# Four-layer graph and expert network on one core: last stage searches in two token halves, third expert stage finishes tiles singly, third graph layer loads bias rows first

## The reference

```python
x = x + _L0_gnn_ref(_layernorm(x), ...)   # and so on, gnn and ffn for 0, 1, 2, 3
```

```python
h = jax.nn.relu(jnp.einsum('bsd,bfd->bsf', x, W1m) + b1m[:, None, :])
res = x + jnp.einsum('bsf,bdf->bsd', h, W2m) + b2m[:, None, :]
mu = res.mean(axis=-1, keepdims=True)
var = res.var(axis=-1, keepdims=True)
return (res - mu) * jax.lax.rsqrt(var + LN_EPS) * lng + lnb
```

```python
Sm = jax.nn.softmax(xf @ W_router + b_router, axis=-1)
G_ek, idx_ek = jax.lax.top_k(Sm.T, k)          # 32 experts, 39 tokens each
tokens = xf[idx_ek]
up = jnp.einsum('gjkh,ghf->gjkf', tok_g, W_up) + b_up[:, None, None, :]
Eout = jnp.einsum('ekf,efh->ekh', silu(up), W_down) + b_down[:, None, :]
y = zeros.at[idx_ek.reshape(-1)].add((G_ek[..., None] * Eout).reshape(-1, H))
```

## Time and profile before

| | us |
|---|---|
| median of 3 runs | 2931.55 (2931.22 to 2933.32) |
| profiled execution, its own time | 2929.89 |
| its span (first to last instruction) | 2928.1 |
| PE busy | 2461.4 (84%) |
| DVE busy | 1624.7 (55%) |
| ACT busy | 837.2 (29%) |
| POOL busy | 585.8 (20%) |
| mean DMA rate over the span | 150 GB/s |

### The profile page before, as it was taken

How to read it: one execution, slowest core, us unless ns; L and a number is a source line. 1 busy time by engine, 2 the same in 40 slices (tenths; PEclk the granted TensorE clock), 3 DMA queues, 4 the chain that set the end, 5 groups by cost and what they waited for, 6 DMA issues and landing times. The chain is left out here.

```text
span 2928.1 us, 31276 instructions
## 1 busy us (share of the span) xinstructions
PE 2461.4 (84%) x10766; PEld 1562.6 (53%) x10766; DVE 1624.7 (55%) x3768; ACT 837.2 (29%) x1860; POOL 585.8 (20%) x563
## 2 busy tenths in 40 slices
PE   3899947999957999985568899999999869958877
PEld 1355446999944777774443455344554434434443
DVE  9999353132424889986246898627963354431100
ACT  0155011111112776771111465105641110101110
POOL 0000065455303555420110000000000101012211
PEclk9899957999977999996789999999999989979988
DMA  4000363776724555543443553214541331459996
GB/s 135 0 1 27 120 187 100 260 230 217 260 73 131 155 156 155 152 88 128 125 137 121 194 193 106 89 62 138 189 132 54 127 138 46 144 195 337 347 347 222
DMA packets 195434, 440.43 MB, mean 150 GB/s; under 512 B 25179, under 2 KB 45387, under 8 KB 194798
## 3 DMA queue, kind: packets, MB, share of 16 engines
q1 hardware_dynamic: 156958, 344.67, 35.1%
q0 software_dynamic: 38320, 93.76, 12.3%
HBM read 394.21 MB, written 43.93 MB: 150 GB/s over the span
## 5 line engine op out<-in xcount | busy, mean ns | idle before, releaser
L2124 PE MATMUL psum<-x_res,HH 125*128 125x512 f32 (+1 forms) x960 | 351.7, 525 | 20.2 <-DVE x_res L2314 20.2
L2124 PEld LDWEIGHTS psum<-x_res,HH 125*128 125x128 f32 x960 | 181.3, 193 | 179.8 <-issue 156.4
L1101 POOL DMA_INDIRECT recd<-edge_records,edge_slots x160 | 193.1, 1207 | 293.8 <-issue 287.2
L1468 POOL DMA_INDIRECT hg<-HT,srcidx x196 | 191.2, 975 | 258.5 <-PE psum L1589 128.6
L1630 ACT ACTIVATE hg<-hg,ex 128x129 f32<-128x129 f32 x784 | 235.2, 389 | 1.6
L1589 PE MATMUL psum<-hg,Dh 128*125 128x258 f32 x784 | 208.0, 424 | 6.8 <-DVE ACC L1531 4.3
L2114 PE MATMUL psum<-W,XO 128*125 128x512 f32 x480 | 209.0, 596 | 0.0
L2891 PE MATMUL psum<-wd,XN 128*40 128x512 f32 (+1 forms) x550 | 162.3, 621 | 31.6 <-DMA wd<-in_L_ffn_b_down 22.2
L1589 PEld LDWEIGHTS psum<-hg,Dh 128*125 128x125 f32 x784 | 160.1, 209 | 40.7 <-issue 6.8
L1135 PE MATMUL psum<-xgT,w 128*128 128x187 f32 x1024 | 172.8, 329 | 4.1 <-DMA w<-in_L_ffn_w 4.1
L1135 PEld LDWEIGHTS psum<-xgT,w 128*128 128x128 f32 x1024 | 166.2, 194 | 8.7 <-DMA w<-in_L_ffn_w 5.8
(11 more groups left out here) (520 smaller groups left out, 3977.0 us busy)
## 6 DMA issues: line engine op xcount, KB each, us to landing
w<-in_L_ffn_w SPq DMA_DIRECT2D x64, 1024.0 KB, 15.1
wd<-in_L_ffn_W_down SPq DMA_DIRECT2D x24, 2560.0 KB
MK<-CT SPq DMA_DIRECT2D x80, 625.0 KB, 3.8
wu<-in_L_ffn_W_up SPq DMA_DIRECT2D x8, 2730.0 KB, 16.4
wd_ahead<-in_L_ffn_W_down SPq DMA_DIRECT2D x6, 2560.0 KB
rows<-ROWS POOLq DMA_DIRECT2D x24, 625.0 KB, 7.2
w<-in_L_ffn_W SPq DMA_DIRECT2D x18, 512.0 KB
t<-in_L_ffn_tv_W SPq DMA_DIRECT2D x16, 512.0 KB
```

What stands on the lines that cost most here:

```text
L1101: pool.indirect_dma_start(out=g.recd, out_offset=bass.IndirectOffsetOnAxis(ap=g.posi[:, c:c + 1], axis=0), in_=g.E8[:, c, :], in_offset=No ...
L1468: pool.indirect_dma_start(out=hg[j % RING][:, c, :], out_offset=None, in_=g.HT, in_offset=bass.IndirectOffsetOnAxis(ap=g.srcidx[:, j * CH ...
L2124: return pe.matmul(flat[:, at:at + x1 - x0], HH[:, k, h * DH + c * 128:h * DH + c * 128 + 128], z[n % 4][:, x0:x1], start=(k == 0 and i < ...
```

## The change

Three edits that don't touch each other.

1. gnn2: the two loads of the bias rows are issued ahead of the mask and W1.
2. ffn2: `dve_group` and `dve_finish` are replaced by `dve_tile`, which finishes one tile after the other on DVE. ACT keeps only the square roots, one column each, and its pass over the tile is gone; the subtraction of the mean and the product with gamma are one instruction that reads PSUM, and the scaling and the sum with X another.
3. last_layers: the search. Tiles t and t + 5 of the routing weights are put beside each other (`self.at`), so that one transposition of 64 columns makes the rows of both halves: expert e of the first 625 tokens in row e, of the second in row 32 + e. Each half gives its largest 40. The list of the second half is turned around in its first 39 places; then slot j of the result is the larger of entry j of the first list and entry j of the turned second list, which together are the largest 39. Slot 40 is gathered still, but the scatter moves 39 rows. Some small tiles are placed in other rooms (`st` in g.ones, `choice` in g.iota_tp).

```diff
@@ class Router @@
+        self.at = list(range(NT))
...
+        self.at = [2 * (t % (NT // 2)) + t // (NT // 2) for t in range(NT)]
...
-        for t in range(NT):
-            ins = pe.transpose(g.PS[0:ne, t // 4, (t % 4) * TP:(t % 4 + 1) * TP], self.L[:, t, :],
-                               g.ident[0:TP, 0:TP])
+        for j in range(NT // 2):
+            ins = pe.transpose(g.PS[0:2 * ne, j // 4, (j % 4) * TP:(j % 4 + 1) * TP],
+                               self.L[:, 2 * j:2 * j + 2, :].rearrange("p a e -> p (a e)"), g.ident[0:TP, 0:TP])
...
+        for k, (first, second) in enumerate(((self.val, self.rval), (self.idf, self.rid))):
+            pe.transpose(g.PS[0:self.count, k, 0:ne], first[0:ne, :], g.ident[0:ne, 0:ne])
+            ins = pe.transpose(g.PS[0:self.count, 2 + k, 0:ne], second[ne:2 * ne, :],
+                               g.ident[ne:2 * ne, ne:2 * ne])
...
+        dve.tensor_copy(WT[:, 0:4 * TP], g.PS[0:2 * ne, 0, 0:4 * TP]).then_inc(*v.up())
+        dve.tensor_copy(WT[:, 4 * TP:5 * TP], g.PS[0:2 * ne, 1, 0:TP]).then_inc(*v.up())
...
+        dve.tensor_copy(self.rval[ne:2 * ne, 0:n], val[ne:2 * ne, n - 1::-1]).then_inc(*v.up())
+        dve.tensor_copy(self.rval[ne:2 * ne, n:], val[ne:2 * ne, n:]).then_inc(*v.up())
         step(dve.tensor_copy(idf[:], ix[:]))
-        step(dve.tensor_scalar(val[:], val[:], 0.0, None, ALU.max))
-        if self.kept < self.count:
-            step(dve.memset(val[:, self.kept:self.count], 0.0))
+        dve.tensor_scalar(self.rid[ne:2 * ne, 0:n], idf[ne:2 * ne, n - 1::-1], float(N // 2), None,
+                          ALU.add).then_inc(*v.up())
+        dve.tensor_scalar(self.rid[ne:2 * ne, n:], idf[ne:2 * ne, n:], float(N // 2), None, ALU.add).then_inc(*v.up())
...
+        dve.tensor_copy(self.sw[:], v1).then_inc(*v.up())
+        step(dve.tensor_copy(self.diff, t1))
+        dve.tensor_tensor(self.ge, v0, self.sw[:], ALU.is_ge).then_inc(*v.up())
+        step(dve.tensor_tensor(self.diff, t0, self.diff, ALU.subtract))
+        dve.tensor_tensor(self.sw[:], v0, self.sw[:], ALU.max).then_inc(*v.up())
+        step(dve.tensor_tensor(self.diff, self.diff, self.ge, ALU.mult))
+        dve.tensor_tensor(self.si[:], t1, self.diff, ALU.add).then_inc(*v.up())
@@ gnn2 @@
         def sp_program():
+            for l, b in enumerate((b1, b2)):
+                sp.dma_start(br[l * C8:(l + 1) * C8, :], b.rearrange("(c p) -> c p", p=128)).then_inc(*b_in.up(16))
             sp_mask(0)
             sp.dma_start(Wt[:, 0:KC, :], rows_of(W1)).then_inc(*w_in.up(16))
-            for l, b in enumerate((b1, b2)):
-                sp.dma_start(br[l * C8:(l + 1) * C8, :], b.rearrange("(c p) -> c p", p=128)).then_inc(*b_in.up(16))
@@ ffn2 @@
-            for i, (t0, t1) in enumerate(groups):
-                act.wait_ge(*var.at(i + 1))
-                act.activation(rs[:, t0:t1], rs[:, t0:t1], ACT.Sqrt).then_inc(*root.up())
-                act.wait_ge(*ready.at(i + 1))
-                for t in range(t0, t1):
-                    act.activation(XN[0:TP, t, :], g.PS[0:TP, t % 8, :], ACT.Identity, bias=nb[:, t:t + 1],
-                                   scale=rs[:, t:t + 1]).then_inc(*normed.up())
+            for t in range(NT):
+                act.wait_ge(*var.at(t + 1))
+                act.activation(rs[:, t:t + 1], rs[:, t:t + 1], ACT.Sqrt).then_inc(*root.up())
...
+        def dve_tile(t):
             step = Chain(dve, v)
...
+            one, res = slice(t, t + 1), g.PS[0:TP, t % 8, :]
+            dve.wait_ge(*down.at(t + 1))
+            step(dve.bn_stats(st[:, t, :], res))
+            step(dve.bn_aggr(mv[:, t, :], st[:, t, :]))
+            dve.tensor_scalar(rs[:, one], mv[:, t, 1:2], EPS, None, ALU.add).then_inc(*var.up())
+            dve.scalar_tensor_tensor(XN[0:TP, t, :], res, mv[:, t, 0:1], lng[:], ALU.subtract,
+                                     ALU.mult).then_inc(*normed.up())
+            dve.wait_ge(*root.at(t + 1))
+            dve.reciprocal(rs[:, one], rs[:, one]).then_inc(*ready.up())
+            dve.wait_ge(*normed.now())
+            dve.wait_ge(*ready.now())
+            step(dve.scalar_tensor_tensor(g.X[:, t, :], XN[0:TP, t, :], rs[:, one], g.X[:, t, :], ALU.mult, ALU.add))
+            tile_statistics(g, t)
@@ last_layers @@
-        rt.slots(SL, K, old[0:NE, 0:N])
+        rt.slots(SL, K, old[0:2 * NE, 0:N // 2], [g.iota_tp[0:SL, k * NE:(k + 1) * NE] for k in range(2)])
...
-                ap=rt.si[:, 0, e:e + 1], axis=0), in_=wo[:, e % (2 * GS), :], in_offset=None,
+                ap=rt.si[0:K, e:e + 1], axis=0), in_=wo[0:K, e % (2 * GS), :], in_offset=None,
```

More of the change, by code:

```diff
@@ L699, in dve_softmax, with slots @@
         dve.wait_ge(*self.v.now())
-    def slots(self, count, keep, WT=None):
+    def slots(self, count, keep, WT=None, choice=None):
         s, ne = self.s, self.ne
         self.count, self.kept = count, keep
[L704 to L710, removed]
+        self.at = [2 * (t % (NT // 2)) + t // (NT // 2) for t in range(NT)]
+        self.WT = WT if WT is not None else s.sb("weights_by_expert", [2 * ne, N // 2])[:]
+        self.ix = s.sb("top_index", [2 * ne, count], U32)
+        self.val, self.idf = s.sb("half_value", [2 * ne, count]), s.sb("half_token", [2 * ne, count])
+        self.rval, self.rid = s.sb("turned_value", [2 * ne, count]), s.sb("turned_token", [2 * ne, count])
+        self.ge, self.diff = choice if choice is not None else [s.sb(n, [count, ne])[:] for n in ("first_half", "between_halves")]
+        self.sw, self.si = s.sb("slot_w", [count, ne]), s.sb("slot_i", [count, ne], I32)
     def pe_slots(self):
@@ L727, in dve_slots @@
         dve, step, g, ne, v = self.g.nc.vector, Chain(self.g.nc.vector, self.v), self.g, self.ne, self.v
[L728 removed]
+        WT, ix, val, idf, n = self.WT, self.ix, self.val, self.idf, self.kept
         dve.nop().then_inc(*self.weights.up())
         dve.wait_ge(*self.turned.at(1))
[L731 to L733 removed]
+        dve.tensor_copy(WT[:, 0:4 * TP], g.PS[0:2 * ne, 0, 0:4 * TP]).then_inc(*v.up())
+        dve.tensor_copy(WT[:, 4 * TP:5 * TP], g.PS[0:2 * ne, 1, 0:TP]).then_inc(*v.up())
         dve.wait_ge(*v.now())
@@ L2569, in dve_merge @@
             dve.nop().then_inc(*w2_in.up())
-        def dve_group(i, t0, t1):
+        def dve_tile(t):
             step = Chain(dve, v)
[L2573 to L2588, removed]
-                dve.tensor_tensor(XN[0:TP, t, :], XN[0:TP, t, :], lng[:], ALU.mult).then_inc(*v.up())
-                dve.wait_ge(*v.now())
-                dve.tensor_tensor(g.X[:, t, :], g.X[:, t, :], XN[0:TP, t, :], ALU.add).then_inc(*v.up())
-                dve.wait_ge(*v.now())
-                tile_statistics(g, t)
+            one, res = slice(t, t + 1), g.PS[0:TP, t % 8, :]
[11 more added lines that the diff above has]
+            tile_statistics(g, t)
         def dve_program():
@@ L2601, in dve_program @@
             dve.wait_ge(*lnb_in.at(1))
-            dve_group(0, *groups[0])
-            for i in range(len(groups)):
-                if i + 1 < len(groups):
-                    dve_group(i + 1, *groups[i + 1])
-                dve_finish(i, *groups[i])
+            for t in range(NT):
+                dve_tile(t)
         sp_program()
@@ L2649, in last_layers @@
         inv, minus = s.sb("inv", [TP, NT]), s.sb("minus_inv", [TP, NT])
-        st, mv, rs = s.sb("st", [TP, NT, 6]), s.sb("mv", [TP, NT, 2]), s.sb("rs", [TP, NT])
+        st, mv, rs = view(g.ones, TP, 0, NT, 6), s.sb("mv", [TP, NT, 2]), s.sb("rs", [TP, NT])
         vectors = s.sig("vectors_loaded")
@@ L2986, in dve_rows @@
                     dve.wait_ge(*scattered.at(16 * (e - 2 * GS + 1)))
-                dve.tensor_scalar(row, g.PS[place[k], 4 + k, :], rt.sw[:, 0, e:e + 1], None,
+                dve.tensor_scalar(row, g.PS[place[k], 4 + k, :], rt.sw[:, e:e + 1], None,
                                   ALU.mult).then_inc(*ev.up())
```

16 lines of the change are left out of this document (5 added, 11 removed).

## The result

The changed kernel took 2903.02 us (median of 4 runs, 2900.26 to 2908.33), the kernel before 2932.44 beside it (4 runs, 2931.22 to 2935.25): a ratio of 0.9906, interval 0.9892 to 0.992. It is 29.4 us faster; 27.5 were forecast (a median of 2904, from 2931.55), and the range of 2898 to 2912 held it. The profiled execution took 2900.26 us with a span of 2898.2, against 2928.1 before.

The account below looks back on a forecast made before the run. Ten barrier-ended stages bound the kernel by what each waits for: bias rows in gnn2, DVE in ffn2, the search in the last. Savings 8.1 + 9.6 + 9.8 = 27.5 us gave 2904 us, range 2898 to 2912.

Parts of the forecast that it names:

- Part 1: gnn2, bias rows first: 7.0 us of PE idleness and 1.9 of clock, less 0.8: 8.1 us saved (6.1 to 8.9).
- the later store: gnn2: POOL's store of attention rows, issued 8.9 us earlier, meets the loads' end; cost 0.8 us, between 0 and 2.8.
- Part 2: ffn2, tiles finished singly on DVE: 3.3 us per tile, 33.1 for ten against 42.7, 9.6 us saved (7.7 to 10.7).
- the root is covered: ffn2: ScalarE's square root runs under DVE's first product (0.74 us); uncovered it would add some 0.3 us per tile.
- Part 3: Last stage, search in halves: 1.0 + 0.8 + 9.2 - 1.2 = 9.8 us saved (8.2 to 10.9).
- the turning: Last stage: PE transposes five pairs of routing-weight tiles instead of ten tiles, saving 1.0 us.
- the copies: Last stage: copies of the turned weights from PSUM fall from 1.72 to 0.93 us, saving 0.8.
- the search: Last stage: fourteen DVE maxima, index searches and replacements over 625 columns, not 1250, save 9.2 us (8.0 to 10.2).
- the merge: Last stage: joining both halves' lists takes seven more small instructions and two more PE transpositions, adding 1.2 us (0.7 to 1.8).
- The copy's slope: Last stage: the PSUM copies' 1.06 ns per column, taken to price search operations at 0.66 us saved each.
- The weight stream: Rival, last stage: the expert-weight stream sets the end by itself, so the search's gain is lost: 2914 us, chance 0.05.
- a fortieth less is nothing: Last stage: scattering 39 rows, not 40, gains nothing; by the skill's rule, 0.2 us per last scatter, half a microsecond overall.

Follow-up runs that it names:

- one pair of kernels: The changed kernel with its 39-row scatters, against the changed kernel with all 40 slots scattered, sent together: 2899.68 and 2905.36 us.

## Why the prediction was right

- **Part 1** gave 7.5 us in the profiled run, 7.9 alone, of the 8.1 forecast, within its 6.1 to 8.9. Idle time (7.0) and clock (1.8) came as worked out; the second was shown by keeping PE busy. The term that was mis-sized is the later store: 0.8 taken, 1.6 measured (4.21 less 2.59), because the traffic that it meets is not only the end of the loads but also the store of X, as the run that holds that store back showed. DVE's first maximum came 7.3 us nearer to the stage's start, where the prediction named 8 to 9. DVE's path, not PE's, sets the end: PE waits for its AB steps, by 1.05 and 2.07 us. That is no sure mark of the change, though: two kernels with the old order show such a wait too (1.87 us in the one with tiles singly, 0.43 in the one with the search in halves).
- **Part 2** gave 9.5 of 9.6 us, at 3.3 us a tile. That the root is covered holds; without that cover it cost 0.27 a tile (the bound said 0.3).
- **Part 3** gave 9.7 of 9.8 us: the turning 1.0, the copies 0.8 (0.67 and 0.27 us), the search 9.1 (2549.07 to 2561.40, against 21.39), the merge 1.1 lost. The copy's slope was the right price for MAX8, which takes 0.80 us.
- **The weight stream** did not set the end by itself: the distance from gather to last scatter did not grow by what the search lost.
- **The scatter** was the wrong sentence: "a fortieth less is nothing" nearly held for one scatter alone on a quiet DMA, while the whole stretch became 3.6 us shorter in one pair of kernels and 1.7 in the pair of before and after. The estimate from the Trainium skill, "DMA: Bandwidth & Descriptors", section "Why a DMA increments its semaphore by 16 and not by 1", of 0.2 us less for each of the last scatters is borne out for the very last one (0.15 between the means); the half microsecond that it gave for the whole was too small, as the gain lies in the stream.
- **Outside the parts** gnn2 was shorter by another 2.3 us. 1.7 of them lie in its last product (L2185 before, L2193 after), 70.59 us against 68.89. The windows of its start, before, then after:

```profile
2180.90:2185.00 4.10, 4.10 (x8) 1.68 (x8) 0.00 (x0) 0.27 (x1) 0.52 (x1) 0.64 1.05 291
```

```profile
2172.60:2177.00 4.40, 4.40 (x12) 1.99 (x12) 0.00 (x0) 0.27 (x1) 0.52 (x1) 1.00 1.04 303
```

The clock was at a mean of 0.64 there and is at 1.00 now. The other traces show that this is chance and not the change. The product takes 70.59 us in eight of the fourteen traces, five of them of kernels with the changed order in gnn2, and 68.89 in six, one of them with the old order. In the same six, PE's first product with the merged weights in ffn2 (L2486 before, L2493 after) takes 19.9 to 20.0 us, with a granted clock of 0.50 in its first 5 us, and 18.8 to 18.9 in the eight (clock 0.62 to 0.64). That is the 0.9 us by which ffn2's start came out longer. Why an execution falls on one side or the other stays open.

The profiled run, 2900.26, came out 2.1 us below the forecast for it (2902.4): part 1 fell short by 0.6, and the scatters gained 1.7 that no term had; 2.3 less in the rest of gnn2 and 0.9 more at ffn2's start are chance, as said. That the median agrees within 1 us is partly luck.

## What to carry to other kernels

Price an edit by the stretch in which it lies, from one landmark to the next before it and after it; three parts added up to 27.1 us that way, and to 36.8 by their medians. Where an idle engine is started earlier, look at what its first transfer now collides with: here that cost 1.6 of 8.9 us, and issuing one bulk store later gave 1.5 back within its stretch. Where a count of rows is changed that a DMA splits, try the number itself: going from 40 rows to 39 is worth 2 to 4 us here, and 37 cost 156 (3055.84 less 2899.68). And before a difference between two traces is put down to an edit, look whether other traces of either kernel show it too: a stretch that no edit touches differed here by over 4 us.

## What the runs showed that was not expected

- A scatter of 37 rows took 11.4 to 12.1 us on a quiet DMA, one of 39 about 4.2 (2886.25 to 2890.45 in the changed kernel). Its issue took 2.29 us, not 1.40. The gathers that stand behind such scatters on POOL came late, and with them the weight loads: a mean of 278 GB/s in place of 348.
- MAX8, FIND_INDEX8 and MATCH_REPLACE8 cost the same: 0.80, 0.80 and 0.79 us for 625 columns on 64 lanes. With 1.45 us for 1250 columns on 32, that is 1.04 ns per column and 0.15 fixed, if the lanes cost nothing. Two copies from PSUM speak for that: 500 columns took 0.662 us on 32 lanes and 0.670 on 64.
- An idle time of 7 us on PE lengthened the 8.6 us of work behind it by 1.8 to 2.4 us (10.41, 10.62 and 11.01 us for the same rows in three kernels with the wait): the loss shows in no row as idleness, only in a longer row and the granted clock.
